# A two-layer graph network on one core: first halves in a buffer of their own, zero rows by partition, receivers' rows in blocks

## The reference, cut to what matters

```python
h = jnp.maximum(_layernorm(x, axis=-1), 0.0)
x = x + _L0_gnn_ref(h, src, dst, edge_attr_3, edge_attr_10, edge_weight, W1, W2)
h = jnp.maximum(_layernorm(x, axis=-1), 0.0)
x = x + _L1_gnn_ref(h, edge_index, Wq, Wk, Wv, Wout)
```

## Time and profile before

| | us |
|---|---|
| median of 3 runs (lowest, highest) | 1405.88 (1405.66, 1410.81) |
| the profiled execution's own time | 1408.44 |
| its span | 1406.6 |
| layer 0, to the last halving on DVE | 0 to 732 |
| between the layers, to the first steps of layer 1 | 732 to 835 |
| layer 1, first part, pairs with a search | 835 to 1047 |
| the 10 groups that follow | 1047 to 1101 |
| softmax, second part | 1101 to 1407 |
| busy: PE, DVE, ACT, POOL | 720.8, 958.7, 646.9, 847.8 |

### The profile page before, as it was taken

One profiled execution on the slowest core, in us unless ns is written; L12 is line 12 of the kernel. 1 busy time (PEld: TensorE's weight loads), 2 busy tenths in 40 slices (PEclk: granted clock), 3 DMA queues, 4 the chain that ended last, 5 costly groups with the idle time before them and its releaser, 6 DMA issues.

```text
span 1406.6 us, 14572 instructions
## 1 busy us (share of the span) xinstructions
PE 720.8 (51%) x4324; PEld 583.7 (41%) x4324; DVE 958.7 (68%) x1692; ACT 646.9 (46%) x1647; POOL 847.8 (60%) x795
## 2 busy tenths in 40 slices
PE   0466666557566666756573523514543179990000
PEld 0355555456455555645462312302321079980000
DVE  6488787877878787887854884615668889991000
ACT  1457666666767567666734554514543122220000
POOL 6776665756657666654005887727663047777775
PEclk9777777867777778767775557657766555555555
DMA  3211111112111112110116438965654000000000
GB/s 68 71 39 45 28 42 49 23 46 81 24 49 38 36 37 61 36 49 22 39 67 156 89 36 63 49 76 64 80 33 31 11 6 12 11 11 10 10 10 8
DMA packets 40515, 60.29 MB, mean 43 GB/s; under 512 B 17347, under 2 KB 30935, under 8 KB 40182
## 3 DMA queue, kind: packets, MB, share of 16 engines
q0 software_dynamic: 25184, 12.32, 15.3%
q1 hardware_dynamic: 12074, 46.84, 10.1%
q10 hardware_dynamic: 3180, 0.21, 0.2%
HBM read 40.33 MB, written 19.36 MB: 42 GB/s over the span
## 4 chain that ended last, share of the span: by engine, by line
DVE 39%; DVEq 14%; PE 12%; DMA 12%; POOL 10%; issue 8%; ACT 2%; SPq 2%; POOLq 0%
POOL out_dram L653 10%; PE sums L1017 9%; DMA src_everywhere<-src_by_columns 6%; DVE h1d_or_products L1353 5%; DMA out_dram<-xin 4%; DVE h1d_or_products L1339 4%; DVE h1d_or_products L1344 3%; DVE dstat L1372 2%; DVE xin L1383 2%; DVE dcen L1378 2%; DVEq L1343 2%; DVEq L1337 2%; DVEq L1312 2%; DVE features_or_scores L1615 1%; DVE h1d_or_products L1440 1%
## 5 line engine op out<-in xcount | busy, mean ns | idle before, releaser
L618 POOL DMA_INDIRECT x_rows<-in_x,src_index x196 | 203.3, 1037 | 159.0 <-PE tens L1011 113.2
L644 POOL DMA_INDIRECT agg_or_stacks<-run_sums,sum_row_index x196 | 217.4, 1109 | 99.0 <-issue 55.2
L653 POOL DMA_INDIRECT out_dram<-agg_or_stacks,scatter_index x196 | 195.4, 997 | 132.3 <-DVE agg_or_stacks L1730 70.8
L618 POOL DMA_INDIRECT x_rows<-in_x,dst_index x196 | 227.6, 1161 | 64.9 <-issue 64.9
L1017 PE MATMUL sums<-h1d_or_products,ident 128*128 128x144 f32 (+1 forms) x896 | 235.0, 438 | 36.8 <-DVE h1d_or_products L1339 29.3
L1353 DVE TENSOR_TENSOR h1d_or_products<-tens,hid 128x768 f32<-128x768 f32 x168 | 157.2, 950 | 106.6 <-PE tens L1011 103.1
L1017 PEld LDWEIGHTS sums<-h1d_or_products,ident 128*128 128x128 f32 x896 | 208.7, 293 | 48.0 <-DVE h1d_or_products L1339 33.0
L1085 PE MATMUL small<-one_column,steps 128*128 128x1 f16 x196 | 37.4, 191 | 156.5 <-DVE steps L1505 110.6
L1007 PE MATMUL tens<-w_scalar_stacks,agg_or_stacks 96*128 96x384 bf16 x196 | 55.1, 367 | 103.5 <-DVE h1d_or_products L1353 103.3
L1007 PE MATMUL tens<-w_scalar_stacks,stack_turned 96*128 96x384 bf16 x196 | 53.8, 359 | 99.9 <-DVE h1d_or_products L1353 99.9
L1085 PEld LDWEIGHTS small<-one_column,steps 128*128 128x128 f16 x196 | 23.9, 122 | 185.0 <-DVE steps L1505 115.3
(11 more groups left out here) (278 smaller groups left out, 2232.2 us busy)
## 6 DMA issues: line engine op xcount, KB each, us to landing
src_everywhere<-src_by_columns SPq DMA_DIRECT2D x14, 896.0 KB, 7.4
xin<-in_x SPq DMA_DIRECT2D x27, 449.5 KB
out_dram<-xin SPq DMA_DIRECT2D x27, 449.5 KB
x_rows<-in_x,src_index POOLq DMA_INDIRECT x196, 2.5
x_rows<-in_x,dst_index POOLq DMA_INDIRECT x196, 3.8
run<-run_sums SPq DMA_DIRECT2D x1, 3136.0 KB, 12.5
agg_or_stacks<-run_sums,sum_row_index POOLq DMA_INDIRECT x196, 7.0
out_dram<-agg_or_stacks,scatter_index POOLq DMA_INDIRECT x196, 2.1
```

The costliest lines, as they stand in the source:

```text
L618: nc.gpsimd.indirect_dma_start(xs[:, t, side, :], None, x, bass.IndirectOffsetOnAxis(ap=idx[:, t:t + 1], axis=0)).then_inc(s_gath[g % LEAD ...
L644: nc.gpsimd.indirect_dma_start(aggr[:, t, :], None, rs, bass.IndirectOffsetOnAxis(ap=ridx[:, t:t + 1], axis=0)).then_inc(s_rsg[g % LEAD2], 16)
L653: nc.gpsimd.indirect_dma_start(out, bass.IndirectOffsetOnAxis(ap=sidx[:, t:t + 1], axis=0), aggr[:, t, :], None, bounds_check=N - 1, oob_i ...
```

## The change

- `halve` writes into a new buffer `first_half`, so DVE's next `multiply` need not wait for `sum_first`; `halve` itself waits for the `sum_first` of the group before. `sum_first` moves into the next group, between chunks 3 and 4 of the turning, and `sum_rest` is done in one piece. Products 4 and 5 now stand together. The buffer shares its space (`late`) with `steps` and `stat_d`.
- There are 128 rows of zeros, and a source without a sum gets row `NONE_ROW + p` in partition p. `decode` takes both constants from `no_row`.
- In layer 1 SP loads slice d + 2 two groups after it stored slice d, with the spread of the next chunk between the two.
- The receivers' rows are done in 7 blocks of 28 columns: blocks 0 and 1 between the layers, blocks 2 to 6 at groups 0, 4, 8, 12, 16 (`dst_centre` on DVE, `dst_square` on ACT), their variances two groups later. `dst_deviation` moves from group 1 to 21, `prepare` from 19 to 24.

```diff
-    rs = nc.dram_tensor("run_sums", [P * T + 1, FEAT], F32, kind="Internal").ap()
+    rs = nc.dram_tensor("run_sums", [P * T + P, FEAT], F32, kind="Internal").ap()
...
+    NB = 4
+    BW = NB * GA
+    NBLK = NG // NB
...
+        late = sb("halves_or_steps", [P, CT * P // 2 + 4 * T])
+        first_half = part(late, 0, 2 * TACT, HID // 2, OG)
...
-                    if SLICE2[g] + 2 < ND:
-                        load(SLICE2[g] + 2)
+                if g - 2 in SLICE2 and SLICE2[g - 2] + 2 < ND:
+                    load(SLICE2[g - 2] + 2)
...
                 if past(g, 0):
-                    sum_rest(g - 1, 0)
+                    sum_first(g - 1)
                 turn_units(g, b, range(4, NCH))
                 if past(g, 0):
-                    sum_rest(g - 1, 1)
+                    sum_rest(g - 1)
...
                 product(g, b, 4)
-                sum_first(g)
-                if more:
-                    turn_units(g + 1, 1 - b, range(1))
                 product(g, b, 5)
                 if more:
-                    turn_units(g + 1, 1 - b, range(1, 2))
+                    turn_units(g + 1, 1 - b, range(2))
                 product(g, b, 6)
...
             def halve(g):
                 v.drain()
-                v.tensor_tensor(prod[:, 0:2 * TACT, 0:HID // 2, :], prod[:, 0:2 * TACT, 0:HID // 2, :],
+                if past(g, 0):
+                    dve.wait_ge(s_sumA, g)
+                v.tensor_tensor(first_half, prod[:, 0:2 * TACT, 0:HID // 2, :],
                                 prod[:, 0:2 * TACT, HID // 2:, :], ALU.add).then_inc(s_half, 1)
...
-                v.scalar_tensor_tensor(found_f[:, 0], found_f[:, 0], float(-1 - NONE_ROW), found_f[:, 1], ALU.add, ALU.mult)
+                v.scalar_tensor_tensor(found_f[:, 0], found_f[:, 0], no_row[:, 1:2], found_f[:, 1], ALU.add, ALU.mult)
...
+            def dst_centre(j):
+
+                at = cols(x1d, j, BW)
+                v.tensor_tensor(at, at, cols(run, j, BW), ALU.add)
+                v.drain()
+                v.tensor_reduce(cols(stat_d[:, 0, :], j, BW), at, AX, ALU.add)
+                v.drain()
+                v.scalar_tensor_tensor(cols(h1d, j, BW), at, float(FEAT),
+                                       spread(cols(stat_d[:, 0, :], j, BW), 2, [P, BW, FEAT]),
+                                       ALU.mult, ALU.subtract).then_inc(s_dc, 1)
...
+                if g % NB == 0 and g // NB + 2 < NBLK:
+                    dst_centre(g // NB + 2)
+                if g % NB == 2 and g // NB + 2 < NBLK:
+                    dst_variance(g // NB + 2)
```

84 lines of the change are left out of this document (42 added, 42 removed).

## The result

The changed kernel takes 1255.29 us, the median of 4 runs (1252.06 to 1258.64), beside 1405.77 us for the kernel before (1405.01 to 1410.81). The ratio is 0.8923, with a 95% interval of 0.889 to 0.8956. The forecast was 1252 us in a range of 1228 to 1300. The profiled execution of the changed kernel took 1253.9 us, with a span of 1252.1, so 154.5 us less than the profiled one of before; the sum had 155.

What follows compares the result with a forecast made beforehand. DVE, waiting for PE's order, was taken to bound layer 0, and late spreads the first part of layer 1, with POOL's gathers as next floor. -91 - 64 = -155 on 1408.4 gives 1253; forecast 1252 us, range 1228 to 1300.

Steps and rivals of the forecast that it cites:

- Products 4 and 5 together: Layer 0: DVE's 103.1-us wait for product 5 goes; with 8 and 4 us given back, -91 us.
- late sums: Layer 0: DVE waits for sums that PE now does later; 0 to 84 us possible, 8 us taken.
- second rival: Layer 0: PE becomes the bound if the sums run at the slow clock; +45 us, 1297 us, chance 15%.
- Zero rows by partition: Layer 1, first part: with 128 zero rows the gathers' queue should not form, so spreads land in time.
- first rival: Layer 1: the zero rows were not the cause, spreads take some 20 us; +22 us, 1272 us, chance 20%.
- "slower" rival: Layer 1: spreads meet a queue that never drains since POOL no longer pauses; 1460 us at 42 us each, chance 3%.
- SP's order: Layer 1: the spread is issued right behind the steps, past store and load; with the spread landing in time, -48 us.
- Receivers' rows in blocks: Start of layer 1: eight DVE operations of 28 columns instead of 98, -20 us; moved blocks lengthen later pairs.
- POOL as the floor: Layer 1, first part: POOL's gathers end the stage at 1039 instead of 1101, -62; DVE's sum -67; -64 taken.
- The lock on the port: Layer 1: shorter DVE operations hold POOL less; five stretched gathers would give back up to 12 us.

Runs made afterwards that it cites:

- e7: The changed kernel with the first sum back between products 4 and 5, its own buffer kept: 1348.57 us, 91.6 us slower than the changed kernel run beside it.
- e5: The changed kernel with one zero row for all sources without a sum, the rest new: 1293.77 us, 36.8 us slower than the changed kernel beside it.
- e6: The changed kernel with SP's old order (load right behind store), zero rows by partition kept: 1257.77 us, 0.8 us above the changed kernel beside it.
- e3: The changed kernel with one zero row and SP's old order, on a slower chip: 1408.28 us beside 1457.92 for the kernel before.
- e1: The changed kernel with one zero row for all sources without a sum, on a slower chip: 1402.48 us beside 1457.92 for the kernel before.
- e4: The changed kernel with receivers' rows in two halves ahead of the first sources, on a slower chip: 1407.2 us, ratio 0.966 to the kernel before.
- c1: The changed kernel again, unedited, as a control: 1257.01 us, ratio 0.8903 to the kernel before.
- e2: The changed kernel with SP's old order, zero rows by partition kept, on a slower chip: 1400.47 us beside 1457.92 for the kernel before.
- e11: The changed kernel with receivers' rows in two halves ahead of the first sources, on another slower chip: 1430.16 us, ratio 0.9698 to the kernel before.
- e8: The changed kernel with one zero row and SP's old order, on a slower chip: 1436.4 us beside 1472.72 for the kernel before.

## Why the prediction was right, point by point

*Products 4 and 5 together: right, and shown by e7.* The sum had -91 for layer 0; measured are 93.6 us ahead of the first gather, and 91.6 us come back when the sum is put back. Of the 103.1 us of the wait, 7.8 remain, in 13 waits of at most 1.0 us. The 8 us for late sums were 6.3, and half of them is one wait in the last group (3.2 us), where no other work lies ahead. Such waits were 7.1 us in the kernel before, so in balance nothing was given back, and 5.4 of the 93.6 us are not the place of the sum (e7). The second rival, PE as the bound, did not come because its condition did not: the rest of the sums never ran at the slow clock, in any group with complete records. That is the reason which the prediction gave for taking 8 us, and it held further than it assumed. It was no safe bet: four of the six waits for sums, 0.26 to 0.87 us, stand behind a first sum that took 2.8 us or more, where the fast ones took 2.18. The rival's price had a slip: 28 x 1.7 is 48, of which 8 stand in the sum already, so +40 and not +45.

*Zero rows by partition: the mechanism right and shown by e5, the size too small.* Of the two ends for one gather, 2.6 and 18.6 engine-us, the low one was taken; counted in the same way as these, the stretch of 870 to 875 us gives 0.07 x 16 x 5 / 4 = 1.4 engine-us each. The share of 0.27, over the stage and over its pairs with a search (719 to 883 us) alike, is under the 0.4 forecast. The first rival, that the row does not matter, falls with e5: the same packets take 17.9% of the engines' time against 6.2%. The Trainium skill's page "DMA: Bandwidth & Descriptors", section "Why small descriptors are slow (HBM only)", which puts the price of a small packet down to fixed overheads per packet and per descriptor, has no word of the address (that it does not matter was the prediction's reading); here the address decides, and the measurement goes before the page. What was mis-sized is that rival's term "spreads take some 20 us, +22": one zero row costs 36.8 us. Spreads take up to 35.5 us in e5 instead of 24.3. A likely reason, not tested by itself, is that POOL pauses less: it waits 20.0 us for the compare in e5 and waited 41.2 before, so the crowded queue is fed more steadily. That would be the mechanism of the "slower" rival, at the near end of its scale.

*SP's order: right only in company.* The prediction took order and zero rows in one term of -48. Alone, the order is worth 0.8 us, with the zero rows in place (e6). With one zero row it should be worth more: four waits of 69.1 us in all became 42.0 in e5. Those two kernels differ in the blocks too, and the clean comparison fell on other chips (5.8 us, e3 against e1). That share stays open.

*Receivers' rows in blocks: the moves right, the worth not shown.* The first steps of layer 1 come 58.5 us behind the first gather (forecast 60 to 61; before 81), the pairs take 21.3 and 15.1 us (forecast 21.2 and 14.6). On a chip of the first kind the parts measured give 91.6 + 36.8 + 0.8 = 129.2 of 153.9 us (1410.94 - 1257.01). The 24.7 us that are left belong to the blocks, to what the order is worth beside one zero row, and to the buffer with the rest in one piece (5.4 us ahead of the first gather, by e7); they were not separated.

*POOL as the floor: right for the last gather, while at the end DVE is as near.* The floor was 217.4 + 55.2 = 272.6 us from the first gather to the issue of the last, 1027 us; in the time of before the last now starts at 935.63 + 93.62 = 1029. The stage gained 62.6 us, between the floor's 62 and DVE's 67, of which the sum took 64. Both limits were real: DVE waits only 3.3 us for gathers in the changed kernel, and in e6 not at all, as told there.

*The lock on the port: the long gathers are gone, what came back is open.* The prediction left up to 12 us to shorter operations of DVE. From 719 us on no gather lasts over 1.9 us, where one took 4.02 in the earlier trace rows. Yet between these two kernels the gathers' mean is 1105 ns instead of 1109: counted above 0.945 us each, the 196 gathers lose 31.4 us now and lost 32.2 before. The two kernels differ in more than the length of DVE's operations, though. POOL waited 41.2 us for the compare before and 3.0 us now, so more of its gathers meet DVE at work. On the chip of e1 to e4 the halves cost 6 to 8 us of gather time. So shorter operations seem to give back a part of the 12 us; on a chip of the first kind it was not measured. The Trainium skill's page "SBUF — State Buffer", section "SBUF: two separate sides", has the lock held for a whole instruction. The trace agrees: the longest gather, 6.33 us, began at 671.79, within the 6.69-us multiplication (L1573) of 670.61, and ended 0.8 us behind it, as its like of 7.24 us did before.

## What to carry to other kernels

Where an engine waits a few microseconds at one place of every group, look at what stands in front of the awaited instruction on the other engine, and whether that work has a deadline at all: here 92 us hung on one sum that nobody needed for another half a group. Look as well at the clock at which the moved work will run: behind each other, the sums took 148 us instead of 213. When a queue is crowded at few GB/s, look at the addresses: let indices that mean "nothing" point to different rows. And measure parts of a change alone and together, beside the same kernel on the same chip: the order of the transfers was worth nothing that could be told once the queue was free.

## What the runs showed of the hardware that was not expected

*Many reads of one row.* A gather of 128 rows of 128 bytes costs some 12.5 engine-us more when most of its reads go to one row than when they go to 128 neighbouring ones (e5 against c1; 9.1 on the chip of e1 and e2). What in the memory makes it so was not looked into; how many of the 128 reads go to that row was not counted, and between 1 and 128 rows nothing was tried.

*Chips on which waits for PE end late.* In three of the four lots the kernel before took 1458 to 1475 us instead of 1406. Instructions there last as long as elsewhere (the multiplication L1364 949 ns in e2 as in the changed kernel, the gathers 1093 ns in e2 against 1105), and the mean granted clock is 0.66 to 0.69 as well. What is longer are waits, for work of PE above all, and not in layer 0 alone: from the scales to the end these chips take 342 to 349 us, where the first kind takes 306 to 308. A group of e11 (its lines are two lower; ACT's copy is L760 as in the changed kernel), PE, ACT and DVE:

```profile
354.38 0.56 PE L1006 MATMUL turnA<-identb,agg_or_stacks 128*96 128x128 bf16 x7
354.78 2.82 PE L1030 MATMUL sums<-h1d_or_products,ident 128*128 128x192 f32 x16
357.44 0.49 PE L1020 MATMUL tens<-w_scalar_stacks,agg_or_stacks 96*128 96x384 bf16 x2
```

```profile
360.69 0.90 ACT L760 COPY agg_or_stacks<-turnA 96x896 bf16<-96x896 bf16 x1 [4.87 <-remote]
```

```profile
360.85 0.33 DVE L1430 TENSOR_TENSOR vmix<-sums,features_or_scores 128x168 f32<-128x168 f32 x1 [1.85 <-remote]
```

By the records PE does the turning from 354.38 us on and the rest of the sums until 357.6, and starts the next product at 357.44. ACT copies what was turned at 360.69 and DVE reads the sums at 360.85, both after a wait whose end the profile can't ascribe. In the group of the changed kernel above, the turning of 334.84 was copied at 335.44. The late sums and turnings then do hold up DVE: in e8 they show as 26.9 + 22.3 + 14.5 us of waits. This is the second rival of the prediction, on those chips, from another cause than the clock. They take the place of the wait that the change removes, which is probably a part of why the versions tried there gain 2 to 4% and not 11%. The cause of the late ends was not found.
